# A PixArt block on one core: order of the beginning and of the drain changed, and seven products that nobody reads

## The reference, cut to what matters

```
shift_a, scale_a, gate_a, shift_m, scale_m, gate_m = split(silu(c) @ W_mod + b_mod, 6)
q, k, v = split(modulate(ln(x), shift_a, scale_a) @ W_qkv + b_qkv, 3)
x = x + gate_a * (softmax(q k^T * scale) v @ W_proj + b_proj)
q_c = ln(x) @ W_qc + b_qc;   k_c, v_c = split(ln(context) @ W_kvc + b_kvc, 2)
x = x + softmax(q_c k_c^T * scale) v_c @ W_cproj + b_cproj
x = x + gate_m * (gelu(modulate(ln(x), shift_m, scale_m) @ W_mlp1 + b_mlp1) @ W_mlp2 + b_mlp2)
```

## Time and profile before

| | |
|---|---|
| median of 3 runs | 376.72 us |
| profiled execution | 376.17 us, its span 374.2 us |
| mean granted TensorE clock | 0.968 |
| busy | PE 338.9 us (91%), ACT 269.7 (72%), DVE 264.0 (71%), POOL 210.0 (56%) |

### The profile page before, as it was taken

One profiled execution on the slowest core, in us unless ns is written; L12 is line 12 of the kernel. 1 busy time (PEld: TensorE's weight loads), 2 busy tenths in 40 slices (PEclk: granted clock), 3 DMA queues, 4 the chain that ended last, 5 costly groups with the idle time before them and its releaser, 6 DMA issues. The chain is left out here.

```text
span 374.2 us, 16029 instructions
## 1 busy us (share of the span) xinstructions
PE 338.9 (91%) x5888; PEld 231.2 (62%) x5888; DVE 264.0 (71%) x671; ACT 269.7 (72%) x526; POOL 210.0 (56%) x479
## 2 busy tenths in 40 slices
PE   4578778999899999999999999998888799999996
PEld 3455545677676777767777676776655355554444
DVE  6965768787788889788888888987866824443401
ACT  2336565888888788887888888887775746776673
POOL 6862677777778677787777778667374300112100
PEclk9955999999999999999999999999999989999999
DMA  5744464434344344434434444344243100101111
GB/s 131 158 102 134 123 149 99 104 92 114 91 104 114 86 100 98 113 90 113 101 72 110 104 100 114 86 102 102 65 102 88 45 3 3 30 28 56 28 28 56
DMA packets 65788, 33.13 MB, mean 89 GB/s; under 512 B 8471, under 2 KB 65495, under 8 KB 65751
## 3 DMA queue, kind: packets, MB, share of 16 engines
q1 hardware_dynamic: 63847, 32.36, 35.6%
q10 hardware_dynamic: 1904, 0.27, 0.6%
HBM read 4.83 MB, written 2.10 MB: 19 GB/s over the span
## 5 line engine op out<-in xcount | busy, mean ns | idle before, releaser
L862 DVE TENSOR_REDUCE mx<-wide 128x8 f32<-128x1024 f32 x64 | 78.2, 1222 | 23.7 <-PE wide L1345 23.3
L1078 ACT ACTIVATE p_c<-wide 128x1024 f32<-128x1024 f32 x64 | 65.5, 1024 | 24.8 <-PE wide L1356 23.8
L1078 ACT ACTIVATE p_s<-wide 128x1024 f32<-128x1024 f32 x64 | 65.6, 1026 | 10.5 <-PE wide L1356 10.5
L862 DVE TENSOR_REDUCE mxc<-wide 128x8 f32<-128x616 f32 x64 | 50.8, 793 | 6.5 <-PE wide L1345 6.2
L1367 PE MATMUL ps_o<-p_s,v_m 128*32 128x128 f32 x1024 | 42.6, 285 | 0.2
L1367 PE MATMUL ps_o<-p_c,vc_m 128*32 128x128 f32 x1024 | 42.2, 283 | 0.1
L1345 PE MATMUL wide<-qk_st 62*128 62x128 bf16 x512 | 26.5, 226 | 9.2 <-DVE mx L862 4.6
L1345 PEld LDWEIGHTS wide<-qk_st 62*128 62x128 bf16 x512 | 15.2, 97 | 25.1 <-DVE mx L862 13.1
L1408 PE MATMUL wide<-m_nT,w_sb 128*128 128x512 f32 x64 | 30.2, 602 | 0.2 <-DVE mxc L862 0.2
L1367 PEld LDWEIGHTS ps_o<-p_s,v_m 128*32 128x32 f32 x1024 | 25.0, 111 | 7.6 <-issue 2.1
L1367 PEld LDWEIGHTS ps_o<-p_c,vc_m 128*32 128x32 f32 x1024 | 24.6, 110 | 6.8 <-issue 0.5
(11 more groups left out here) (182 smaller groups left out, 812.9 us busy)
## 6 DMA issues: line engine op xcount, KB each, us to landing
qk_st<-qkp SPq DMA_DIRECT2D x94, 128.0 KB, 2.5
qkc_st<-qkcp SPq DMA_DIRECT2D x90, 128.0 KB, 2.5
out<-m_out SPq DMA_DIRECT2D x7, 256.0 KB, 2.3
xs<-x SPq DMA_DIRECT2D x3, 512.0 KB, 4.8
qk_st<-nmT SPq DMA_DIRECT2D x64, 4.0 KB
qkc_st<-nmcT SPq DMA_DIRECT2D x64, 4.0 KB
ctx_sb<-ctx SPq DMA_DIRECT2D x3, 308.0 KB
w_sb<-L_xcond_W_mlp SPq DMA_DIRECT2D x2, 256.0 KB, 3.1
```

Source lines behind the costliest of these rows:

```text
L862: nc.vector.reduce_max(mxt[:, b].rearrange("q (x r) -> q r x", r=2)[:, r], src, AX.X, negate=True).then_inc(sems[done], 1)
L1078: nc.scalar.activation(dst[u % 2][:].rearrange("k x q -> k (x q)"), ps_st[:].rearrange("k s x -> k (s x)"), ACT.Exp, scale=SCALE).then_inc ...
```

## The change

In the beginning: x of pair 0 is loaded ahead of w_mod, and the third piece of x no longer before the first stacking DMAs but after the stack of pair 0 is complete. The six modulation products are split: two at once, two behind the first transposes of x, two behind `rows_v`. `tables(range(2))` and `head_columns` come after pair 0's normalisation instead of before, `tables(range(2, 6))` after `first_keys` inside `gate_rows`. GpSimd's block of copies and memsets moves from the end of slot -1 to the end of slot 0. The first four spreads move from slot 0 to the end of slot -1 on both engines, and the other four are made in beats 0 and 1. TensorE gets seven products whose result nobody reads (`unread`, a 128x256 float32 product): four into `ps_max` behind the second `rows_qk` and ahead of the wait for `g3_set`, and one into `ps_o` in each of the beats 2, 3 and 4 of slot 0.

In the drain: on VectorE `m_modulate(1, 1)` comes right behind `m_normalise(1, 1)`, and the maxima of the last pair are taken from there on, with the moments of group 2 between the second and the third and its normalisation behind the fourth. On GpSimd the first split of the last pair's maxima comes before `m_rstd_step(2)`. On TensorE `m_transpose(1, 1)` comes before the last part of `m_up(0, 0)`.

```
@@ -412,8 +412,8 @@
...
             sp.dma_start(cond_sb[:], cond).then_inc(sems["cond_in"], 16)
+            load_x(0)
             sp.dma_start(wmod_sb[:], w_mod).then_inc(sems["wm_in"], 16)
-            load_x(0)
             sp.dma_start(wqkv_sb[:], w_qkv).then_inc(sems["wq_in"], 16)
@@ -429,7 +429,6 @@
...
                 halves(3, b_kvc, 0, "bc_in")
-            load_x(2)
 
@@ -504,6 +503,7 @@
...
                     load_c(1)
+                    load_x(2)
                 if s == 0:
@@ -703,7 +703,7 @@
...
                     nc.gpsimd.memset(qkcp[:].bitcast(u32), 0).then_inc(sems["pad_set"], 1)
-                if a and a.first():
+                if h and h.first():
                     pool.wait_ge(sems["wc_in"], 16 * 2)
@@ -739,9 +739,9 @@
...
             split_max(p14, 1, mxc, nmc, "mxc_set", "nmch_set", "nmc_set", "mtc_ps")
+            split_max(p15, 0, mxc, nmc, "mxc_set", "nmch_set", "nmc_set", "mtc_ps")
             m_rstd_step(2)
-            for b in range(G):
-                split_max(p15, b, mxc, nmc, "mxc_set", "nmch_set", "nmc_set", "mtc_ps")
+            split_max(p15, 1, mxc, nmc, "mxc_set", "nmch_set", "nmc_set", "mtc_ps")
             with pool.Fori(3, NGRP) as g:
@@ -795,10 +795,11 @@
...
 
+                normalise("x", second, x_of(second), "xt_ps")
+                first_keys()
+                tables(range(2, 6), 2)
                 dve.wait_ge(sems["mod_set"], 2)
                 nc.vector.tensor_copy(gsrc[:, 0:B], mod[:, 2])
-                normalise("x", second, x_of(second), "xt_ps")
-                first_keys()
                 dve.wait_ge(sems["bo_ps"], 1)
@@ -951,9 +952,6 @@
...
                     if t == 0 and far:
-                        if far.first():
-                            tables(range(2), 1)
-                            head_columns()
                         if a and a.first():
@@ -968,7 +966,8 @@
...
                         if far.first():
-                            tables(range(2, 6), 2)
+                            tables(range(2), 1)
+                            head_columns()
                     if t == 6 and d:
@@ -1019,12 +1018,14 @@
...
             m_normalise(1, 1)
+            m_modulate(1, 1)
+            cross_maxima(p15, [0])
+            residual(p13, "projc_ps", "proj_c", "x2_set")
+            cross_maxima(p15, [1])
             w(dve, "x2_set", 6)
             m_moments(2)
-            m_modulate(1, 1)
+            cross_maxima(p15, [2, 3])
             m_normalise(2, 0)
-            residual(p13, "projc_ps", "proj_c", "x2_set")
-            cross_maxima(p15, range(NU))
             cross_out(p14)
@@ -1210,9 +1211,9 @@
...
                         sums(d, "s", ps_o, "pv_ps", "sum_set", "ot_ps")
-                    if t < NU and h and h.first():
+                    if t < 2 and h and h.first():
                         for n in range(2):
-                            spread(2 * t + n, ps_st[:, n])
+                            spread(2 * t + n + 4, ps_st[:, n])
                     if t == 4 and a:
@@ -1243,6 +1244,8 @@
...
                     biased(a.shift(1))
+                    for n in range(4):
+                        spread(n, ps_st[:, n % 2])
             slots(act, slot)
@@ -1322,10 +1325,15 @@
...
             pe.wait_ge(sems["wm_in"], 16)
-            for k in range(6):
-                last = mm(ps_max[:, int(k < 2), k * B:(k + 1) * B], wmod_sb[:, k * C:(k + 1) * C], siluT[:], start=True, stop=True)
-                if k in (1, 5):
-                    last.then_inc(sems["mod_ps"], 1)
+
+            def modulation(ks):
+                for k in ks:
+                    last = mm(ps_max[:, int(k < 2), k * B:(k + 1) * B], wmod_sb[:, k * C:(k + 1) * C], siluT[:],
+                              start=True, stop=True)
+                    if k in (1, 5):
+                        last.then_inc(sems["mod_ps"], 1)
+
+            modulation((0, 1))
 
@@ -1482,6 +1490,10 @@
...
                     scores_t(p, u, qkc_st, "stc_ps")
+
+            def unread(dst):
+
+                mm(dst[:, 0:GT], wdh[:, 0], xmT[:], start=True, stop=True)
 
@@ -1584,6 +1596,8 @@
...
                         rows_v()
+                        if a.first():
+                            modulation((4, 5))
                     if t == 4 and h:
@@ -1596,6 +1610,8 @@
...
                         transposed(bank(s, "x_t"), "x", far, T, "xt_ps", GT)
+                        if far.first():
+                            modulation((2, 3))
                     if t == 6 and d:
@@ -1603,9 +1619,11 @@
...
                         flip_out(bank(s, "obc_t"), "c", e, "oc_set", "obct_ps")
-                    if h and h.first() and t < NU:
+                    if h and h.first() and t in (2, 3, 4):
+                        unread(ps_o)
+                    if h and h.first() and t < 2:
                         for n in range(2):
-                            spread(2 * t + n, ps_st[:, n])
+                            spread(2 * t + n + 4, ps_st[:, n])
                     if t == 4 and a and a.first():
@@ -1614,12 +1632,16 @@
...
                         rows_qk(Slot(s.i, s.k + 1))
+                        for _ in range(4):
+                            unread(ps_max[:, 0])
                         pe.wait_ge(sems["g3_set"], 4)
...
                         tr(rows[0:3, 3 * C:4 * C], g3[:, :, 2 * B], ident16[:]).then_inc(sems["g_ps"], 1)
+                        for n in range(4):
+                            spread(n, ps_st[:, n % 2])
 
@@ -1666,9 +1688,9 @@
...
             max_t(after("max_c0", p14, 0), p14, 1, nmc, "nmc_set", "mtc_ps")
-            m_up(0, 0, True, [3])
             after("q_c", p15, 2)
             m_transpose(1, 1, True)
+            m_up(0, 0, True, [3])
             cross_proj(after("obc_t", p13, 1), p13)
...
             w(pe, "m_hT_set", NF)
```

14 lines of the change are left out of this document (8 added, 6 removed).

## The result

The change made the kernel slower. The kernel before took 377.67 us (median of 4 runs beside the changed one), the changed kernel 382.41 (4 runs, 380.49 to 384.16); the ratio is 1.0135 with a 95% interval of [1.0095, 1.0176]: +5.1 us by the ratio (the two medians lie 4.7 apart) where -1.2 was predicted, and outside the range. The profiled execution after took 384.16 us (span 382.3), against 376.17 (span 374.2) before; so the two traces lie 8.1 us apart, more than the kernels do.

The account below looks back on a forecast made before the run. Bound taken: a chain of slots behind the first scores and, in the drain, VectorE's chain into TensorE plus the half clock. Beginning +1.1, drain -2.3, sum -1.2 us: 375.0 profiled, 375.5 median; range 373.6 to 378.6.

Parts of the forecast that it names:

- The drain: End of the kernel: TensorE takes up the last pair's unit 1 earlier and the clock stays up, -2.3 us.
- Rival D: Drain keeps its cold stretch, leaving the beginning's +1.1: 376.6 us; chance 0.10.
- Step 1: Beginning: x loaded ahead of w_mod, so first modulated x at 8.2 us instead of 9.3.
- the stop: Slot -1: TensorE stands from about 12.2 to 14.4 us waiting for VectorE's tables; work behind comes 2.3 later.
- Steps 2 and 3: Slot -1: late tables stop TensorE, delaying work 2.3 us; GpSimd's block leaves, so the cast loses about 2.1 us of blocking.
- step 3: Slot -1: without GpSimd's block the split gate source is ready at about 17.1 us instead of 18.5.
- Step 4: Before slot 0: four unread products cost 2.1 to 4.0 us on the path; first scores at 24.1, +3.6.
- Step 5: Slot 0 at full clock with four fewer spreads: slot 1 starts 12.55 us after first scores, not 14.73, -2.2.
- Step 6: Slot 0: GpSimd's moved block is hidden beside VectorE's context normalisation and memsets, counted 0, bounds 0 to +2 us.
- the sum: Whole kernel: +1.1 us in the beginning and -2.3 in the drain give -1.2 us.
- -0.3: Slot 1, which ran cold until 37.3 us, loses 0.3 us in its first two units.
- Rival C: Beginning: clock not back before the unread products end, first scores at 25.5, time 378.7 us; chance 0.18.

Follow-up runs that it names:

- e1: The drain's reordering alone, on the kernel before; ratio 0.9924 to the kernel before, -2.9 us.
- e14: Changed kernel with ScalarE's last three bias DMAs issued by SyncE instead; ratio 1.0086 to the kernel before.
- e10: Kernel before with only GpSimd's block moved from the end of slot -1 to the end of slot 0; 0.5% slower (+0.51%).
- e7: Changed kernel without the seven unread products and with TensorE's wait for all the modulation moved later; ratio 1.0011 to the kernel before.
- e12: Kernel before with only the seven unread products added; ratio 1.0022 to the kernel before.
- e13: Kernel before with only the loads of x reordered; ratio 0.9974 to the kernel before.
- e15: Kernel before with the drain's reordering, the new order of loads and three bias DMAs moved to SyncE; ratio 0.9946 to the kernel before.
- e11: Kernel before with only the first four spreads moved to slot -1; ratio 1.0013 to the kernel before.
- e8: Like e7, with GpSimd's block also back at the end of slot -1; ratio 1.0058 to the kernel before.
- e2: Changed kernel with the drain of before, so the beginning's edits alone; ratio 1.0123 to the kernel before, +4.6 us.
- e4: Changed kernel with GpSimd's block of copies and memsets back at the end of slot -1; ratio 1.0045 to the kernel before.
- e5: Changed kernel with TensorE's wait for all the modulation moved from before the bias products to before the unread ones; ratio 0.9999 to the kernel before.
- e6: Changed kernel with only GpSimd's four weight copies back in slot -1, memsets still in slot 0; ratio 1.0130 to the kernel before.
- e3: Changed kernel without all seven unread products; ratio 0.9995 to the kernel before.
- e9: Kernel before with only the new order of modulation products, tables and head_columns; ratio 1.0104 to the kernel before.

## Why the prediction was wrong, by its own steps

**The drain (predicted -2.3) was right.** From unit 0's scores to the end of the third down product it took 10.92 us before and 8.24 after, -2.7 for that execution; unit 1 followed by 1.24 where 1.4 was named; no low window. Alone it gives 0.76% (e1). Rival D is out.

**Step 1 failed.** x was normalised at 5.97 (predicted 6.2), the transposes went early (6.37, predicted 6.6), and yet the modulated x started at 8.51 and ended at 9.3, as before, where an end at 8.2 was forecast. ScalarE issued bias DMAs on its own queue until 8.40, in the kernel before until 8.24, and its compute stood behind them. Its timeline had that row before the change; I had read ScalarE's compute rows alone:

```profile
7.76 0.48 ACTq L1072 DMA_DIRECT2D bo_sb<-L_xcond_b_mlp  x1
```

e14 takes the bound away and meets the next one, the copies of `head_columns`, which the change itself had moved beside a memset of GpSimd. The forecast of 1.1 us of gain, which was to pay for half of the stop, was 0.

**Steps 2 and 3 were right as mechanisms.** The stop of TensorE ended at 15.23 with VectorE's tables, the second projections came at 17.76 (predicted 16.7, the lost 1.1 of step 1), the cast took 0.20, the gate source was ready at 17.8 (predicted 17.1). ScalarE's stacking DMAs landed 2.5 us after their issue, and pair 0's stack was complete at 20.0, both as predicted. What I had not drawn is that in the kernel before step 3 has nothing to win: the first scores wait for DMAs, and e10 turns 2.0 us of earlier gate rows into a wait of 3.88.

**Step 4 held.** The products took 2.38 us inside 2.1 to 4.0, the gate transposes came at 21.91 against 21.3, first scores at 24.67 against 24.1. By the durations the clock rose near 20, as the step assumed (20.3); half of the 1.1 us that step 1 lost was made good here, 4.15 us from the second projections to the gate transposes and not 4.6. From 20.0, when the stack was complete, TensorE's own program held the first scores back: products, gate transposes, spreads. First scores came at 19.6 to 20.9 in seven kernels (before, e1, e7, e10, e12, e13, e15), at 22.1 or later in all that had the stop or the products on the path, at 22.02 with the early spreads alone (e11), and at 24.75 where the gate cast was held (e8).

**Step 5 failed: slot 0 came out 1.2 us longer than forecast.** From the first scores to the first exponential scores the forecast holds (8.51 us, predicted 8.4; units every 1.75 us, at clock 1.00). Then the clock fell, at 34.3, and the exponential scores of units 1 to 3 and the values of all four ran at the half level: slot 1 came 13.77 us after the first scores and not 12.55. TensorE had been idle for 3 of the 8.5 us before, although the three unread products (0.60 to 0.70 us each) lay in them. Taking the clock from where it stood at 23 us and holding it for 15 more was the step: my bounds knew a clock that comes late, not one that falls again. The unread products don't prevent it: each of the seven traces that have them (after, e2, e4, e5, e6, e12, e14) shows a fall between 16 and 36 us. Where it comes differs between kernels that hardly differ (e3 28 to 39, e5 27 to 41, e7 none until 59, e13 none before 372), and no order of the beginning tried here was shown to control it. It also differs between executions of one kernel: the mean granted clock of the 122 executions of the kernel before that stand beside the experiments runs from 0.955 to 1.000. The 44 of them below 0.98 took 379.1 us on average, the other 78 took 378.8, and the changed kernel's four have the same mean clock as these 122, 0.981. So the fall in slot 0 is shown for one execution, and a lower clock doesn't account for the 5.1 us.

**Step 6 failed, and is the largest miss that the runs put a price on.** The block in slot 0 was counted at 0 with bounds to +2. The context normalisation takes 3.43 us there, and in every kernel with any of the block in slot 0 (after, e2, e3, e5, e6, e7, e10, e14) 3.4 to 4.3 us, in every other 0.60. In the changed kernel slot 1's first maximum then starts 1.3 us behind its scores (before 0.7). e10 against before puts the block's move at 0.5%, 1.9 us, and e4 against the changed kernel at 0.9%, 3.4 us; e8 against e7 shows no gain from moving it back. The Trainium skill's page "SBUF — State Buffer", section "Who interferes with whom", which the prediction had set aside, names just these operations as blocked while the other engine holds the shared ports; the trace agrees that one engine's work holds the other's, and shows more: two pairs of instructions that take 0.60 and 0.56 us alone took 3.43 and 3.35 side by side, not 1.2 one after the other.

**What the sum left out.** The two traces differ by 8.1 us: 3.8 at the first maximum of slot 1, 5.9 more in slots 1 to 5, 3.0 less from there to the last `m_y`, 1.4 more behind it. So the largest part stands where the prediction had nothing but -0.3 and a block counted at 0. In slot 1 (2.1 us longer) the third maximum came 5.27 us after the first and not 3.80, with the clock low until 44.5 and not 37.3. In front of slots 2 and 3 TensorE waited 1.07 and 2.26 us for the DMAs that stack the pair; before, 0.49 and 0.38. Such waits are in most traces and differ from one to the next: slots 1 to 5 took 79.3 us together in the kernel before and 79.4 to 83.4 in the others with the block in slot -1, and 80.7 to 85.2 where some of it lies in slot 0 (e10 and e11 left out). That these groups differ by more than their scatter isn't shown, and it stays open how much of the 5.1 us arises there. The effects don't add up either: without the products, without the stop, or with the block back, the changed kernel is 1.4, 1.4 and 0.9% faster, yet without both products and stop it is 1.2% faster. What each edit is worth depends on the others, or the 4 runs of the changed kernel put it too high; the runs don't decide. Rival C (378.7, the clock not back before the products' end) had the sign but not the mechanism: the clock was back at the first scores.

## What to carry to other kernels

Before moving work to the front, find what ends the last wait in front of the first full-rate stage. Here it was a chain of DMAs: the 2.0 us that e10 won upstream of it were hidden, and the stop of e9 came out as later first scores. An engine that also issues DMAs has these in its program order: read its queue rows with its compute rows when asking how early it can start. When copies, casts or memsets of GpSimd are moved, look for VectorE's copies, casts and scalar operations at the new place, for there each can take several times its time.

## What was not expected of the hardware

- VectorE and GpSimd held each other for longer than the sum of their work: 3.43 and 3.35 us (0.60 and 0.56 apart) in the changed kernel. Beside the rest of the block VectorE's instructions were stretched too: 3.31 to 3.58 us for three instructions of 0.14 to 0.23 in e9; 4.06 for a cast of 0.20 in e8.
- The place and number of the low-clock stretches differ from trace to trace with the same work on TensorE: 3.2 us of it in all in e13, 25.1 in the kernel before, which differ by the order of a few loads. The mean clock differs as much among executions of one kernel, 0.955 to 1.000, and time follows it weakly (0.3 us between the 44 lowest and the others).
- From the last `m_y` to the end of the span it took 3.9 to 4.0 us in 15 traces and 5.3 and 5.1 in the changed kernel and e14: 1.4 us of the 8.1 between the two profiled spans is that, at the very end.
